# Causal attention of a fused layer: scores and maximum products in 64-row halves of TensorE, first loads from two queues

## The reference

```
q = _rms(heads(wq), qn_w)
k = _rms(heads(wk), kn_w)
v = heads(wv)
scores = jnp.einsum('bhqd,bhkd->bhqk', q, k) * HD ** (-0.5)
causal = jnp.tril(jnp.ones((T, T), bool))
scores = jnp.where(causal[None, None], scores, -jnp.inf)
attn = jax.nn.softmax(scores, axis=-1)
ao = jnp.einsum('bhqk,bhkd->bhqd', attn, v)
```

## Time and profile before

| | us |
|---|---|
| median of 3 runs | 2724.9 |
| lowest and highest of them | 2722.4, 2728.35 |
| the profiled execution, its own time | 2727.49 |
| its span, first to last instruction | 2725.6 |
| PE busy in the span | 2474.7 (91%) |
| DVE busy | 1943.2 (71%) |
| ACT busy | 1275.9 (47%) |
| mean granted TensorE clock | 0.973 |

### The profile page before, as it was taken

The page is one execution under the profiler, slowest core; times in us unless marked ns, Lnnn a source line. Parts: engine busy times, 40 slices in busy tenths (PEclk is TensorE's granted clock), DMA queues, the critical chain, the costliest instruction groups (busy, mean ns, idle before and its releaser), DMA issues. The chain is left out here.

```text
span 2725.6 us, 66903 instructions
## 1 busy us (share of the span) xinstructions
PE 2474.7 (91%) x26336; PEld 1758.1 (65%) x26336; DVE 1943.2 (71%) x3759; ACT 1275.9 (47%) x1945; POOL 180.2 (7%) x350
## 2 busy tenths in 40 slices
PE   5998888989888985799999999999869999999999
PEld 4777777777777774233333333333259999999998
DVE  6877777777777773798888888888256565655554
ACT  3333333333333330356666666666634545454454
POOL 0000000000000002111101101111160000000000
PEclk9999999999999997899999999999979999999999
DMA  2010000000101001211201101100030101010100
GB/s 74 14 29 22 22 22 22 22 23 24 25 23 26 22 18 38 72 44 36 59 21 47 55 21 51 46 23 13 18 115 20 37 20 38 19 38 19 38 19 27
DMA packets 138281, 90.11 MB, mean 33 GB/s; under 512 B 68544, under 2 KB 130624, under 8 KB 138048
## 3 DMA queue, kind: packets, MB, share of 16 engines
q1 hardware_dynamic: 136448, 81.34, 10.5%
q0 software_dynamic: 1600, 5.24, 0.6%
HBM read 56.89 MB, written 29.36 MB: 32 GB/s over the span
## 5 line engine op out<-in xcount | busy, mean ns | idle before, releaser
L1279 DVE TENSOR_REDUCE a_mx<-a_pm 128x1 f32<-128x512 f32 (+3 forms) x1120 | 702.4, 671 | 127.0 <-PE a_pm L1177 69.9
L1261 ACT ACTIVATE a_pt<-a_sc 128x1024 f32<-128x1024 f32 (+3 forms) x640 | 540.9, 896 | 338.2 <-PE a_sc L1197 337.6
L1177 PE MATMUL a_pm<-a_ka,a_qa 96*128 96x512 bf16 (+3 forms) x1280 | 401.0, 354 | 16.5 <-DMA a_qa<-q_scratch 11.5
L1197 PE MATMUL a_sc<-a_qa,a_ka 98*128 98x512 bf16 (+3 forms) x1280 | 338.1, 349 | 30.6 <-ACT a_pt L1261 19.5
L1177 PEld LDWEIGHTS a_pm<-a_ka,a_qa 96*128 96x128 bf16 x1280 | 124.0, 97 | 314.0 <-DVE a_mx L1279 216.7
L1217 PE MATMUL a_po<-a_pt,a_v_st 128*32 128x512 f32 (+3 forms) x2560 | 300.9, 542 | 0.8 <-POOL a_pt L1145 0.7
L1804 DVE TENSOR_TENSOR e_h_lo<-v_all,e_h_hi 128x512 fp32r<-128x512 f32 x208 | 148.6, 716 | 188.7 <-ACT e_h_hi L1651 187.5
L1197 PEld LDWEIGHTS a_sc<-a_qa,a_ka 98*128 98x128 bf16 x1280 | 110.5, 98 | 155.2 <-ACT a_pt L1261 61.8
L1649 ACT ACTIVATE v_all<-e_ps 128x512 f32<-128x512 f32 x176 | 103.5, 588 | 125.7 <-PE e_ps L1541 124.6
L1145 POOL TENSOR_SCALAR_AFFINE_SELECT a_pt<-a_pt 128x256 f32<-128x256 f32 x256 | 102.5, 406 | 750.7 <-ACT a_pt L1261 748.1
L1541 PE MATMUL e_ps<-e_h_hi,e_e_l_hi 128*128 128x256 f32 x512 | 147.6, 288 | 0.0
(11 more groups left out here) (311 smaller groups left out, 5392.5 us busy)
## 6 DMA issues: line engine op xcount, KB each, us to landing
a_ka<-k_scratch SPq DMA_DIRECT2D x192, 64.0 KB, 2.3
a_qa<-q_scratch SPq DMA_DIRECT2D x192, 64.0 KB, 2.3
o_scratch<-a_o_sb SPq DMA_DIRECT2D x32, 256.0 KB, 2.6
v_all<-o_scratch SPq DMA_DIRECT2D x256, 32.0 KB
q_scratch<-r_q_part SPq DMA_DIRECT2D x192, 32.0 KB, 1.5
k_scratch<-r_k_part SPq DMA_DIRECT2D x192, 32.0 KB, 1.6
r_x_tok<-in_x SPq DMA_DIRECT2D x32, 128.0 KB, 2.1
s_scratch<-r_s_tok SPq DMA_DIRECT2D x32, 128.0 KB, 1.7
```

Of the source, the lines that this page charges most:

```text
L1177: last = mm(out[:, at_:at_ + width], qa[b][0:NP, qc, h0 + i, 128 * (qt % 4):128 * (qt % 4) + 128], ka[b][0:NP, h0 + i, 512 * kc:512 * kc + ...
L1197: last = mm(sc[x][:, y, off:512], ka[b][:, h, 128 * j:128 * j + 128], qa[b][:, qc, h, off:512], start=True, stop=True)
L1261: nc.scalar.activation(pt[x][g % 2][:, :, off:512], sc[x][:, :, off:512], ACT.Exp).then_inc(s_p[x], 1)
L1279: ve.tensor_reduce(mx[:, h0:h0 + heads, qt, kc:kc + 1].rearrange("p h o -> p (h o)"), pm[:, k % RING, 0:heads * width].rearrange("p (h w) ...
```

## The change

The contraction is cut in two planes of at most 64 rows. Plane 0 (`MAIN`, 64 rows) has four pairs of parts, plane 1 (`REST`, 34 rows) the other two and the two rows of the maximum. Of each two heads, the even one lies in partitions 0 to 63 and the odd one in 64 to 127, so a product uses one half of the array's rows, and its neighbour in the stream the other half.

- Scores: four products for a head pair in place of two: plane 0 of both heads, then plane 1 of both, accumulated.
- Maximum units: only plane 0 (64 rows) is multiplied, four of the six pairs, so that the maximum that is subtracted is that of slightly rounded scores (softmax does not depend on it). The mask is two 64-row products for each head in place of one of 128 rows. A narrow diagonal unit holds at most two heads of the same half, so the 128-column blocks give two units in place of one: 1152 units in all where there were 1120.
- Loads: each of the 12 transfers of a chunk becomes two, one for each half, of half the size (384 for k and q each in place of 192), and `load_rows` issues four in place of two. ACT's queue issues the second halves of chunks 0 and 1 of iteration 0.
- Order on SP: for iteration 0 the chunks' loads are due at -10, -9, -0.4 and 1, so `load_rows(0, 0)`, due at -0.5, comes ahead of chunks 2 and 3. All other due steps are as before, so the 96 transfers of iteration 1 still stand ahead of `load_rows(0, 2)`.
- The constant table grows by 128 columns and the mask tile on chip doubles; the memsets of the rows of ones are cut in two.

```diff
-PARTS_Q, PARTS_K = (0, 0, 0, 1, 1, 2), (0, 1, 2, 0, 1, 0)
-NP = 6 * AD
-NROW = NP + 2
+PARTS_Q, PARTS_K = (0, 0, 1, 1, 0, 2), (0, 1, 0, 1, 2, 0)
+MAIN = 4
+REST = 2 * AD + 2
+
+def rows_of(h, n):
+    return slice(64 * (h % 2), 64 * (h % 2) + n)
...
-                heads = 512 // width
-                for h in range(0, 4, heads):
+                heads = 2 if width <= 256 else 1
+                for h in range(0, 4 if heads == 1 else 2):
...
-        qa = [sb(f"qa{b}", [NROW, QC, 4, 512], BF16) for b in range(B)]
-        ka = [sb(f"ka{b}", [NROW, 4, T], BF16) for b in range(B)]
+        qa = [sb(f"qa{b}", [128, 2, QC, 2, 512], BF16) for b in range(B)]
+        ka = [sb(f"ka{b}", [128, 2, 2, T], BF16) for b in range(B)]
...
                     for r, k in enumerate(parts):
-                        src = io[n + "_dram"][k, b, u * 64:u * 64 + 64, tok]
-                        sp.dma_start(to[AD * r:AD * r + AD, :, :], src.rearrange("(h d) t -> d h t", d=AD)
-                                     ).then_inc(s_load[b][c], 16)
+                        src = io[n + "_dram"][k, b, u * 64:u * 64 + 64, tok].rearrange("(i y d) t -> y d i t", y=2, d=AD)
+                        for y in range(1 if it == 0 and c < 2 else 2):
+                            at_row = 64 * y + AD * (r % MAIN)
+                            sp.dma_start(to[at_row:at_row + AD, r // MAIN, :, :], src[y]).then_inc(s_load[b][c], 16)
...
                 for k in range(2):
-                    sp.dma_start(qa[b][NP + k:NP + k + 1, c, :, :].rearrange("o h (q t) -> o (h q) t", t=128),
-                                 mrow[:, c, k, :]).then_inc(s_mload[b][c], 16)
+                    for y in range(2):
+                        at_row = 64 * y + 2 * AD + k
+                        sp.dma_start(qa[b][at_row:at_row + 1, 1, c, :, :].rearrange("o h (q t) -> o (h q) t", t=128),
+                                     mrow[8 * y:8 * y + 8, c, k, :]).then_inc(s_mload[b][c], 16)
...
-                    events.append((freed if it >= B else -10 if it == 0 else 3 + c, 0, it, c))
+                    events.append((freed if it >= B else (-10, -9, -0.4, 1)[c] if it == 0 else 3 + c, 0, it, c))
...
+                        rows = rows_of(h0, 64)
                         for i in range(heads):
-                            last = mm(out[:, at_:at_ + width], qa[b][0:NP, qc, h0 + i, 128 * (qt % 4):128 * (qt % 4) + 128],
-                                      ka[b][0:NP, h0 + i, 512 * kc:512 * kc + width], start=True, stop=kc != qc,
-                                      skip_group_check=True)
-                            if kc == qc:
-                                last = mm(out[:, at_ + width - 128:at_ + width], ident16, neg_qk, start=False, stop=True,
-                                          skip_group_check=True)
+                            last = mm(out[:, width * i:width * i + width],
+                                      qa[b][rows, 0, qc, h0 // 2 + i, 128 * (qt % 4):128 * (qt % 4) + 128],
+                                      ka[b][rows, 0, h0 // 2 + i, 512 * kc:512 * kc + width], start=True, stop=kc != qc,
+                                      tile_position=(rows.start, 0), skip_group_check=True)
+                            for half in range(2 if kc == qc else 0):
+                                last = mm(out[:, width * i + width - 128:width * i + width], cb16[rows, 0, half, :],
+                                          cb16[rows, 1, half, :], start=False, stop=half == 1,
+                                          tile_position=(rows.start, 0), skip_group_check=True)
...
-                for y in range(2):
-                    h = 2 * x + y
-                    last = mm(sc[x][:, y, off:512], ka[b][:, h, 128 * j:128 * j + 128],
-                              qa[b][:, qc, h, off:512], start=True, stop=True)
+                for part, n in enumerate((64, REST)):
+                    for y in range(2):
+                        rows = rows_of(y, n)
+                        last = mm(sc[x][:, y, off:512], ka[b][rows, part, x, 128 * j:128 * j + 128],
+                                  qa[b][rows, part, qc, x, off:512], start=part == 0, stop=part == 1,
+                                  tile_position=(rows.start, 0), skip_group_check=True)
...
+            for c in range(2):
+                tok = slice(512 * c, 512 * c + 512)
+                for to, n, parts in ((ka[0][:, :, :, tok], "k", PARTS_K), (qa[0][:, :, c, :, :], "q", PARTS_Q)):
+                    for r, k in enumerate(parts):
+                        src = io[n + "_dram"][k, 0, 0:64, tok].rearrange("(i y d) t -> y d i t", y=2, d=AD)
+                        at_row = 64 + AD * (r % MAIN)
+                        act.dma_start(to[at_row:at_row + AD, r // MAIN, :, :], src[1]).then_inc(s_load[0][c], 16)
```

More of the change, by code:

```diff
@@ L1039, in attention_phase @@
         const = lambda name, lo=0, hi=None: cst[:, at[name][0] + lo:(at[name][0] + hi if hi is not None else at[name][1])]
-        cb16 = sb("masks", [128, 2, 128], BF16)
-        qa = [sb(f"qa{b}", [NROW, QC, 4, 512], BF16) for b in range(B)]
-        ka = [sb(f"ka{b}", [NROW, 4, T], BF16) for b in range(B)]
+        cb16 = sb("masks", [128, 2, 2, 128], BF16)
+        qa = [sb(f"qa{b}", [128, 2, QC, 2, 512], BF16) for b in range(B)]
+        ka = [sb(f"ka{b}", [128, 2, 2, T], BF16) for b in range(B)]
         v_st = [sb(f"v_st{b}", [128, KTS, 4, 32]) for b in range(B)]
@@ L1060, in attention_phase @@
         last_unit = {e[1:3]: k for k, e in enumerate(entries) if e[0] == "U"}
-        s_load = [[sig(f"loaded{b}{c}", 1, 16 * 12).sem for c in range(QC)] for b in range(B)]
-        s_mload = [[sig(f"m_loaded{b}{c}", 1, 16 * 2).sem for c in range(QC)] for b in range(B)]
+        s_load = [[sig(f"loaded{b}{c}", 1, 16 * 24).sem for c in range(QC)] for b in range(B)]
+        s_mload = [[sig(f"m_loaded{b}{c}", 1, 16 * 4).sem for c in range(QC)] for b in range(B)]
         s_ostore = [sig(f"o_stored{c}", 1, 16).sem for c in range(QC)]
@@ L1122, in values, with ones @@
                                       ).then_inc(s_vst[b], 1)
-            nc.gpsimd.memset(ka[0][NP:NROW, :, 0:512], 1.0).then_inc(s_kones, 1)
-            pool.wait_ge(s_kones, 1)
+            def ones(b, tok):
+                for y in range(2):
+                    at_row = 64 * y + 2 * AD
+                    nc.gpsimd.memset(ka[b][at_row:at_row + 2, 1, :, tok], 1.0).then_inc(s_kones, 1)
+            ones(0, slice(0, 512))
+            pool.wait_ge(s_kones, 2)
             for b in range(B):
@@ L1130, in _ @@
             pool.wait_ge(s_vst[0], 1)
-            nc.gpsimd.memset(ka[0][NP:NROW, :, 512:T], 1.0).then_inc(s_kones, 1)
-            pool.wait_ge(s_kones, 2)
+            ones(0, slice(512, T))
+            pool.wait_ge(s_kones, 4)
             values(1)
             pool.wait_ge(s_vst[1], 1)
-            nc.gpsimd.memset(ka[1][NP:NROW, :, :], 1.0).then_inc(s_kones, 1)
-            pool.wait_ge(s_kones, 3)
+            ones(1, slice(0, T))
+            pool.wait_ge(s_kones, 6)
             pool.wait_ge(s_one, 1)
@@ L1156, in _ @@
             mm = nc.tensor.matmul
-            ident16, neg_qk = (cb16[:, i, :] for i in range(2))
             def maxima(ks):
@@ L1191, in scores @@
                 if j == 0 and x == 0:
-                    pe.wait_ge(s_mload[b][qc], 32 * (u + 1))
+                    pe.wait_ge(s_mload[b][qc], 64 * (u + 1))
                 if g:
                     pe.wait_ge(s_p[x], g)
-                for y in range(2):
-                    h = 2 * x + y
-                    last = mm(sc[x][:, y, off:512], ka[b][:, h, 128 * j:128 * j + 128],
-                              qa[b][:, qc, h, off:512], start=True, stop=True)
+                for part, n in enumerate((64, REST)):
+                    for y in range(2):
+                        rows = rows_of(y, n)
+                        last = mm(sc[x][:, y, off:512], ka[b][rows, part, x, 128 * j:128 * j + 128],
+                                  qa[b][rows, part, qc, x, off:512], start=part == 0, stop=part == 1,
+                                  tile_position=(rows.start, 0), skip_group_check=True)
                 last.then_inc(s_sc[x], 1)
@@ L1223, in _ @@
             pe.wait_ge(s_ones, B)
-            pe.wait_ge(s_kones, 1)
+            pe.wait_ge(s_kones, 2)
             scores(0, 0)
@@ L1269, in _ @@
             ve.memset(mx[:, :, :, :], -3e38)
-            for i, name in enumerate(("ident", "neg_qk")):
-                last = ve.tensor_copy(cb16[:, i, :], const(name))
+            for i, name in enumerate(("ident_halves", "neg_halves")):
+                last = ve.tensor_copy(cb16[:, i, :, :].rearrange("p k c -> p (k c)"), const(name))
             last.then_inc(s_one, 1)
@@ L1289, in _ @@
                         before, b = divmod(it - 1, B)
-                        dve.wait_ge(s_mload[b][qc], 32 * (before + 1))
+                        dve.wait_ge(s_mload[b][qc], 64 * (before + 1))
```

20 lines of the change are left out of this document (11 added, 9 removed).

## The result

The changed kernel takes 2707.0 us (median of 4 runs, 2705.5 to 2711.1), the kernel before 2723.7 beside it (4 runs): ratio 0.9942, 95% interval 0.9924 to 0.9959. It is faster by 0.6%, clear of the noise: 16.7 us where 54 were forecast. The profiled execution took 2705.8 us, its span is 2704.1.

What follows compares the result with a forecast made beforehand. PE's stream was taken to set the step, with DVE close below. From the profiled 2727.5 us, -75 (halves) + 16 (stall) + 5 (clock) gave 2673.5, or 2671 as median; own range 2640 to 2695, wider range 2603 to 2715.

Steps and rivals of the forecast that it cites:

- part 2: Split transfers on SP: start 3.9 us earlier, then a stall before step 12, +16 us, and lost clock, +5 us.
- The total of 16 + 5 = 21 us: Start of the attention phase: 16 us from the stall before step 12, 5 us from half clock after it.
- part 1: Products in halves, long attention stretch: the halves run at the same time, 775 us falls to 700, a gain of 75.
- PE's step: Full step of the long stretch: PE's work falls to 2.41 us, with DVE's at 2.42.
- the 2.55 forecast: Sign of being right: PE's full step near 2.55 us, where it was 2.84.
- The step that failed: Long stretch: loss above the limiting engine taken as twice the present 33 us, so 66 us and a stretch of 700.
- a floor of 634: Long stretch: PE's total work after the change, 87 us an iteration over 7.27 iterations, 634 us.
- DVE's floor: Long stretch: 1031 reductions at 0.604 us, adjusted for narrower units and chunk ends, 632 us.
- rival 1: Long stretch: DVE's floor reached or the stall shorter, full step 2.45 us, total about 2605 to 2640; chance 0.20.
- Rival 2: Long stretch: halves idle at each join, full step about 2.70 us, stretch 737, total 2708; chance 0.16.
- Rivals 3, 4 and 5: SP's queue decides, 2746 (chance 0.08); weight loads of a half not hidden, 2792 (0.03); no overlap in bf16, 2986 (0.03).

Runs made afterwards that it cites:

- e12: Changed kernel with every iteration's loads of chunks 0 to 3 due at steps 9, 10, 21 and 22 of the iteration before; 2682.3 us.
- e2: Changed kernel with the loads of iteration 1 due at steps 9 to 12 in place of 3 to 6; 2707.2 us.
- e9: Changed kernel with only iteration 1's loads moved, chunks 0 to 3 due at steps 9, 10, 21 and 22; 2704.4 us.
- e4: Changed kernel with every maximum unit taken from rows 0 to 63, one half of the array; 2780.7 us.
- e5: Changed kernel with each maximum reduction reading only half of its unit's columns; 2710.7 us.
- e7: Changed kernel without the mask products of the maximum units; 2699.8 us.
- e3: Changed kernel with the planner costing narrow steps longer, so that they take more units; 2700.4 us.
- e11: Changed kernel, iteration 1's loads due at 9, 10, 21, 22, narrow steps costed longer, unmasked units of slots 0 to 8 multiplied three times; 2695.6 us.
- e1: Kernel before with only the split transfers and their changed order, products left as they were; 2748.4 us.

## Why the prediction was right and wrong

Right were the sign, the range (2603 to 2715 holds 2707.0), and the mechanism of **part 2**. The first rows and scores: forecast 3.9 us earlier; measured 1092.06 - 1070.51 = 21.6 us behind the first load against 25.2 before, 3.6 earlier. PE then stands still for the rows of chunk 2 behind 96 loads, and the clock is halved behind it.

The total of 16 + 5 = 21 us against 20.9 at step 11 is in part luck, for its two terms missed in opposite directions. The scores of step 12 start 1169.17 - 1070.51 = 98.7 us behind the first load, against 1153.33 - 1074.68 = 78.7 before: 20.0 later, and not 16.0. (The forecast's 1169.3 on the clock of the trace is met only because the phase began 4.2 us earlier in this profile.) The rows of chunk 1 go out 1.4 us later than forecast; the rows of a pair cost 0.67 us each and not 0.57; and 96 loads and a store take 47.6 us in place of 45.6, for a load is 5.57 / 12 = 0.464 us in most rows but up to 6.83 / 12 = 0.57 in some. The clock in turn cost less than 5 us: it is 0.50 until about 1172 and 1.00 from 1174, and between step 12's scores and step 23 the kernel after loses only 1 us more against e12 (17.5 less 16.3), which has no stall there. Not forecast was the slower start: the granted clock was 0.50 up to 1128, and fully back only from 1136.

Part 2 said the cost in later iterations is nothing. After has five more waits for rows in the loop and one in the last chunk, together 3.4 us, the longest 1.4; that they stay so small hangs on the first stall, which gives the queue time. Without it the same twofold number of loads stalls PE at steps 24 or 52 (e2, e9).

Right in **part 1** are the mechanism and PE's step: the halves start together (and e4 undoes the gain), the step without DVE's limit is 2.41 us (e5), and a full step is 2.49, under the 2.55 forecast. (The first reading is off by a little: 0.44 / 2 is 0.220 us a product and not 0.218.) DVE is busy 88% of the long stretch, where above 90% was the sign to look for. Weight loads stayed hidden, though there are twice as many score loads (PEld's rows, from the step after the one shown above):

```profile
1538.08 0.32 PEld L1219 LDWEIGHTS a_sc<-a_qa,a_ka 64*128 64x128 bf16 x4
1538.31 0.34 PEld L1196 LDWEIGHTS a_pm<-a_ka,a_qa 64*128 64x128 bf16 x2
1538.56 0.50 PEld L1219 LDWEIGHTS a_sc<-a_qa,a_ka 64*128 64x128 bf16 x4
```

In e5 a half has six products in a step, 6 x 0.218 + 1.10 = 2.41 us, which is the measured step and leaves no time for the half's six loads of some 0.09 us. In e4 the lower half has eight, 2.84 us, and the step is 2.83. The Trainium skill, page TensorE: Matmul & The Clock Gate, Part 3 (The mechanism), has them overlap only across row groups; the trace disagrees with it again, for by that rule these steps would be 0.5 and 0.7 us longer. (The same section also names a background weight buffer into which a load can be pulled ahead; that would fit.)

**The step that failed** is the last of part 1: "Two equal engines that hand over through three banks must lose more: I take twice, 66 us, so 700 us", on a floor of 634 (DVE's was 632). The stretch is 736.8 us, 102.8 above that floor: 36.8 too long, nearly the whole error (the loop's 36 us of 37). The rest of the sum was close. DVE's floor itself stands: the distance of 0.604 us is 0.60 in the loop too. (DVE is busy 650.6 us there, but a reduction that doesn't follow another directly counts with its whole 0.69 us and not with 0.60.)

The loss doesn't lie where I put it, between equal engines in the full steps. There it is 0.08 us a step, about 1.4 us in the 17 full steps without masks of an iteration, and these gave 4.7 us where 17 x (2.84 - 2.55) = 4.9 follow from the forecast's own 2.55. The forecast's gain of 10.3 us an iteration needed another 5.4 us from the 23 masked or narrower steps, whose PE work I had taken down with the rest, by PE's total. They gave 1.0. The idle time of DVE says the same. The groups by form of e12, of DVE between 1160 and 1900 (e12 because no stall is mixed in):

```profile
L1309 DVE TENSOR_REDUCE a_mx<-a_pm 128x1 f32<-128x512 f32 x818 | 514.4, 684 | 47.2 <-PE a_pm L1196 26.9 <-PE a_pm L1201 17.7
L1309 DVE TENSOR_REDUCE a_mx<-a_pm 128x1 f32<-128x384 f32 x116 | 57.7, 550 | 8.1 <-PE a_pm L1201 7.9
L1309 DVE TENSOR_REDUCE a_mx<-a_pm 128x2 f32<-128x512 f32 x58 | 39.4, 689 | 17.9 <-PE a_pm L1201 17.2
L1309 DVE TENSOR_REDUCE a_mx<-a_pm 128x2 f32<-128x256 f32 x58 | 22.5, 419 | 4.7 <-PE a_pm L1201 4.5
```

Of 77.9 us idle before a reduction, 47.3 end with a mask product (L1201), which is the last of a masked unit. A full step with masks took 3.15 us on average before and takes 3.09. Which engine holds it is not one answer: with half the reduction (e5) it is 2.89, without masks (e7) 2.81, so it gives way to either. Why these steps hardly gain from PE's shorter units stays open beyond that. Some light steps wait for ACT, as the forecast's rival 1 feared (one at 1582.16 leaves DVE 0.91 us idle); PE waits 20.5 us for it in the whole phase, against 19.5 before.

e12 prices the change without the stall: 38.0 us less than before at the end of the phase, 38.1 by the medians. Of this 41.5 us are gained behind step 11 and 3.5 lost in the start; part 1 claimed 75. The gain of e3 shows that a better spread takes back some 7 us at after's order.

Rival 2, "half the gain", gave 2708 and is 1 us off the median, and its stretch of 737 us is the measured one, but for another reason than its own: it wanted a full step of 2.70 us, which is 2.49. The number was right by accident. Of rival 1, the full step of 2.45 is nearly reached, but the time is not. Rivals 3, 4 and 5 are out: the stretch gained 38 us, the full steps are shorter, the halves overlap.

## What to carry to other kernels

When an engine is relieved, cost each kind of step by itself and then add; PE's total over the whole stretch, with one sum for all losses, gave twice the truth here. Don't read a long merged row of an engine as work without a wait: 29 reductions in 18.01 us look like 0.62 us each, and are 0.60 with a wait of 0.08 once a step. And when transfers are split, look at the order on the issuing queue as a whole: doubling the issues moved a stall to wherever two sets of loads met, and a single patch of the order only moved it on (e2, e9), while spreading all loads between the small urgent transfers removed it (e12, 1.4% under the kernel before).

## What the hardware showed

The issue time of a load went by number and not by size: the middle value of the distances on SP is 0.466 us for 32 KB (after) and 0.469 for 64 KB (before), so splitting transfers doubles SP's work.

The granted clock was the surprise. In the kernel before it is 1.00 all through the loop, and at 1.00 already at 1114 us, some 40 us behind the phase's first load. In the kernel after it is 0.50 up to 1128, 1.00 for four us, 0.50 again, and at 1.00 up to the stall only from 1136, 65 us behind the first load:

```profile
1120.00:1126.00 6.00, 5.76 (x31) 1.33 (x31) 3.79 (x6) 4.46 (x5) 0.00 (x0) 0.50 0.26 73
```

PE is busy 5.76 of 6 us there, and at 1.2 GHz. The cause is not shown. e11 speaks for too little work of PE. The wait of 1.0 us before step 4 is not it alone: in e12 the clock had risen to 1.00 at 1109 and was back at 0.50 from 1113, with PE busy in every one of the next us and its wait only at 1119. e1, with products on the full array, held 1.00 from 1113 to 1126 and fell behind a wait of 2.7 us there.

In the loop, too, the clock fell in e2, e5, e7 and e9 (to 0.50 to 0.67 in stretches of 6 us), apart from the long stalls. Each of these falls stands right behind a wait of PE for rows of the maximum of 1.5 to 3.3 us; the kernels with e12's order have no such wait in the loop, and no fall. One wait of 2.2 us in e7 was followed by none, so the wait alone doesn't decide. Whether e5's shorter reductions would pay off with e12's order was not tried.
